# A fused two-layer decoder kernel: the shared LayerNorm steps of its Silu rounds and its last three Gelu visits are put in another order, and GpSimd takes part of the last tile's work

## The chip, the core and the metric

The kernel runs on one core of one Trainium2 chip. The metric is the device time in microseconds (us) of the whole program; before the change it is 501.37 us, the median of three runs (501.33 to 501.39). The core has TensorE (PE in the profile; its weight loads are PEld), VectorE (DVE), ScalarE (ACT), GpSimd (POOL) and SyncE (SP, which only issues DMAs). Each engine works through its own list of instructions in order, and the lists meet in semaphores: an instruction waits until a semaphore has reached a value, and whatever stands behind it on the same engine waits with it.

## The reference

The input is x of 8 x 56 tokens of width 256, a context of 8 x 1500 rows of width 256, and a mask over the context. All is in float32.

```python
x = x + L0_attn(layernorm(x))                # 16 heads of 128, ALiBi, causal
x = x + L0_xattn(layernorm(x), ctx, mask)    # 16 heads of 16 over 1500 rows, LayerNorm of the result
x = x + L0_ffn(layernorm(x))                 # ternary weights, 8-bit activations, silu(gate) * up, Hadamard
x = x + L1_attn(layernorm(x))                # attention over the batch axis: 16 query heads, 4 key heads of 16
x = x + L1_xattn(layernorm(x), ctx)          # LayerNorm(x5n + summary of a decaying scan) * gamma + beta
x = x + L1_ffn(layernorm(x))                 # 1024 wide, round(h / 0.1) clipped, gelu, power-of-two weights
```

Three of these matter here. `L0_ffn` is the one with the Silu. `L1_attn` attends from each of the 8 batch elements at one position to batch elements 0 to b; a token row forms products q x k over up to 8 batch elements, sums them in groups of 16, takes a softmax, and forms products p x v. `L1_xattn` is two LayerNorms in a row: x5 is normalised, the summary is added, that is normalised again, scaled by gamma (`rows_sb[:, 2]`), shifted by beta (`rows_sb[:, 3]`) and added to x.

## The kernel before, in words

The 448 tokens are four tiles of 112 rows (`TT`), each with two batch elements; the tiles are counted 0 to 3. After the first attention the kernel runs one long loop of 48 rounds, `s` = 0 to 47 (`PAIRS`), each for 250 rows of the context. A batch element takes 6 rounds, a tile 12. A round on PE is: scores (L1522), the key projection of a later piece (`project_k`, L1451), the weighted values of the round before (L1540), the value projection (`project_vu`, L1461). ACT takes the exponentials (L628) and most copies out of PSUM; DVE clips the exponentials (L998, `clip`), multiplies the context by the scan's weights (L972, `weigh`), and forms the remainder of each context piece (L832, `remainder`, in odd rounds), which the split float32 products need.

When a tile's 12 rounds are over, its other layers are worked in between the rounds of the next tiles. What belongs to round `o` behind a tile's end stands in small functions `first`, `early`, `between` and `late`, called from fixed places of the round: on ACT `first` comes right behind the exponential and the key copy, `early` further on, `late` last; on DVE `early` stands ahead of the clip, `between` behind it, `late` last.

Three rounds, 16, 28 and 40 (`SILU`), hold the Silu of one tile: ACT loads the Silu table, does the Silu, and loads back the table that has exponential and logarithm. To make room, DVE takes over copies that ACT otherwise does: the value copy (L1009), the rounding of a context piece (L827), and one round later (`BEHIND`, rounds 17, 29, 41) the key copy `take_k` (L1004). In rounds 28 and 40 the second LayerNorm chain of the tile before falls into the same place: `add_summary` on DVE (L1156 to L1159; its variance goes to ACT through `s_var[6]`), `root(6)` on ACT (an Ln and an Exp, L333 and L337), `add_normalised` on DVE (L1163, variance through `s_var[7]`), `root(7)` on ACT, and `normalise7` on DVE (L1168).

Behind round 47 comes the tail, written out by hand: rest of tile 2, all of tile 3, and the last layer of all tiles. It needs the Gelu table for tiles 0 and 1 together, for tile 2, and for tile 3, with the other table between. `keep_warm(n)` (L1731) issues n matmuls whose result nobody uses. Tile 0's last product (L1782, `hidden_part(0)`) waits for its Gelu; `turn_x7` (L1675) turns a tile's last normalised rows for the last layer, `hidden` is L1687, and tile 3's last two products are L1886 and L1893. In `spread` (L1094) and `attend` (L1131) DVE forms tile 3's products for all 8 batch elements, 256 elements for each.

## Time and profile before

| | |
|---|---|
| median of three runs | 501.37 us (501.33 to 501.39) |
| the profiled execution, its own time | 500.37 us |
| span of that execution, first to last instruction | 498.6 us |
| mean granted TensorE clock | 0.992 |
| PE busy | 475.3 us, 95% |
| DVE busy | 365.3 us, 73% |
| ACT busy | 321.6 us, 65% |
| POOL busy | 4.2 us, 1% |

All durations below come from that one execution. What lies outside its span is 1.8 us. A row of the time line gives the start from the span's beginning, the duration, engine, line, operation, what is written and read, and in brackets how long the engine stood idle before it and what ended that. Where several equal instructions are merged, the duration is from the start of the first to the end of the last.

### The profile page before, as it was taken

What the parts mean: (1) busy time and instruction counts of PE and PEld (TensorE: products, weight loads), DVE (VectorE), ACT (ScalarE), POOL (GpSimd) and SP (SyncE); (2) the same over time, 40 slices, a digit from 0 to 9 for tenths busy, and PEclk for the clock granted to TensorE, in tenths of its full rate; (3) what the DMA queues carried; (4) which work ended last, traced back from release to release, by engine and by line L of the source; (5) the groups of instructions that cost most, each with busy time, mean ns of one, the idle gap of its engine ahead of it and who ended that gap; (6) DMA issues with size and microseconds to landing.
All of it is one profiled execution on the core that took longest, in us unless ns stands there. A gap on an engine that the chain in (4) does not pass through costs nothing.

```text
span 498.6 us, 16397 instructions
## 1 busy us (share of the span) xinstructions
PE 475.3 (95%) x7061; PEld 406.9 (82%) x7067; DVE 365.3 (73%) x820; ACT 321.6 (65%) x591; POOL 4.2 (1%) x15
## 2 busy tenths in 40 slices
PE   7999999999989999999999999899999999896897
PEld 7999999999878888878888888788888788684575
DVE  5576887887658755567966579966969975798973
ACT  4677787877566666677566566666667556445644
POOL 1000000000000000000000000000000000000000
PEclk9999999999999999999999999999999999988999
DMA  6376452200501211111111111111111100000000
GB/s 201 108 254 203 168 166 84 64 23 28 206 1 45 79 50 44 44 44 44 44 44 44 44 44 44 44 44 44 42 44 44 44 3 3 3 1 0 1 11 28
DMA packets 12236, 30.86 MB, mean 62 GB/s; under 512 B 1666, under 2 KB 4867, under 8 KB 11396
## 3 DMA queue, kind: packets, MB, share of 16 engines
q1 hardware_dynamic: 11716, 29.08, 18.2%
q8 instruction: 56, 0.92, 0.7%
q0 software_dynamic: 192, 0.51, 0.3%
q10 hardware_dynamic: 256, 0.23, 0.1%
q14 instruction: 16, 0.13, 0.1%
HBM read 29.35 MB, written 0.46 MB: 60 GB/s over the span
## 4 chain that ended last, share of the span: by engine, by line
PE 69%; DVE 20%; ACT 5%; issue 4%; DMA 1%; DVEq 0%; ACTq 0%
PE psb L1461 10%; PE psb L1451 9%; PE psa L1370 8%; PE psa L1522 8%; PE psb L1540 6%; PE psa L1383 4%; PE pst L1392 4%; PE psb L1423 3%; PE psa L1403 2%; ACT shared L628 2%; DVE shared L998 1%; DVE st L782 1%; PE pst L1607 1%; DVE scratch L972 1%; PE psb L1414 1%
## 5 line engine op out<-in xcount | busy, mean ns | idle before, releaser
L1461 PE MATMUL psb<-wkv,cx 128*125 128x256 f32 x576 | 80.3, 288 | 2.7 <-DVE kx L1004 2.7
L1451 PE MATMUL psb<-cx,wkv 128*128 128x500 f32 x276 | 74.5, 405 | 0.8 <-ACT vmem L471 0.8
L1461 PEld LDWEIGHTS psb<-wkv,cx 128*125 128x125 f32 x576 | 71.0, 186 | 4.9 <-DVE kx L1004 3.0
L471 ACT ACTIVATE vmem<-psb 125x512 f32<-125x512 f32 x45 | 26.8, 596 | 50.1 <-PE psb L1461 49.8
L1451 PEld LDWEIGHTS psb<-cx,wkv 128*128 128x128 f32 x276 | 48.3, 188 | 12.6 <-ACT vmem L471 1.1
L1522 PE MATMUL psa<-qb,kx 32*125 32x112 f32 x1536 | 54.7, 279 | 0.8 <-ACT shared L628 0.6
L998 DVE TENSOR_SCALAR shared<-shared,top 125x896 f32<-125x896 f32 x48 | 30.8, 683 | 32.8 <-ACT shared L628 32.6
L1522 PEld LDWEIGHTS psa<-qb,kx 32*125 32x125 f32 x1536 | 46.3, 183 | 8.3 <-issue 3.5
L628 ACT ACTIVATE shared<-psa 125x1792 f32<-125x1792 f32 x24 | 40.0, 1668 | 17.4 <-PE psa L1522 17.2
L1370 PE MATMUL psa<-cx 128*128 128x448 f32 x192 | 44.5, 382 | 0.7 <-ACT cx L362 0.7
L628 ACT ACTIVATE smem<-psa 125x1792 f32<-125x1792 f32 x23 | 38.3, 1667 | 9.4 <-PE psa L1522 9.4
L998 DVE TENSOR_SCALAR smem<-smem,top 125x896 f32<-125x896 f32 x48 | 30.8, 681 | 16.5 <-ACT smem L628 16.0
L1370 PEld LDWEIGHTS psa<-cx 128*128 128x128 f32 x192 | 36.1, 195 | 3.8 <-DVE cx L797 1.0
L972 DVE CUSTOM_DVE_ANT_0 scratch<-ring,cw 128x500 f32<-128x500 f32 x48 | 32.3, 672 | 0.1
L377 ACT ACTIVATE shared<-shared,negmax 112x112 f32<-112x112 f32 x64 | 24.1, 377 | 10.0 <-DVE negmax L872 10.0
L832 DVE TENSOR_TENSOR cx<-ring,cx 128x1000 fp32r<-128x1000 f32 x24 | 28.7, 1194 | 2.5 <-ACT cx L393 2.0
L464 ACT ACTIVATE kx<-psb,cols_sb 128x500 f32<-128x500 f32 x43 | 28.8, 671 | 2.4 <-PE psb L1451 2.2
L1540 PEld LDWEIGHTS psb<-shared,vmem 125*32 125x32 f32 x1536 | 20.4, 110 | 8.5 <-issue 6.9
L1540 PEld LDWEIGHTS psb<-smem,vmem 125*32 125x32 f32 x1536 | 20.3, 110 | 8.0 <-issue 7.7
L1383 PE MATMUL psa<-wkv,cx 128*112 128x256 f32 x192 | 25.2, 280 | 0.0
L1383 PEld LDWEIGHTS psa<-wkv,cx 128*112 128x112 f32 x192 | 24.4, 174 | 0.7
L1540 PE MATMUL psb<-shared,vmem 125*32 125x56 f32 x1536 | 24.1, 214 | 0.3 <-DVE craw L989 0.3
(350 smaller groups left out, 833.7 us busy)
## 6 DMA issues: line engine op xcount, KB each, us to landing
ring<-ctx_t_dram SPq DMA_DIRECT2D x24, 500.0 KB, 3.4
whd<-wqk_dram SPq DMA_DIRECT2D x16, 256.0 KB, 2.7
qb<-wvp_dram SPq DMA_DIRECT2D x8, 256.0 KB, 2.8
whd<-wo_dram SPq DMA_DIRECT2D x16, 128.0 KB, 2.6
wraw<-w_dram SPq DMA_DIRECT2D x2, 1024.0 KB, 5.8
mats_sb<-mats_dram SPq DMA_DIRECT2D x1, 1536.0 KB, 8.1
wraw<-gate_dram SPq DMA_DIRECT2D x1, 1024.0 KB, 6.8
wraw<-up_dram SPq DMA_DIRECT2D x1, 1024.0 KB, 6.5
```

What stands on the lines that cost most here:

```text
L464: nc.scalar.activation(kx[u % 2][:, m, :], bank[:, 0:UT], ACT.Identity, bias=cols_sb[:, 1, m:m + 1]).then_inc(s_ke, 1)
L471: nc.scalar.activation(vu[u % 2][:, 2 * r:2 * r + 2, :, 0:XD], bank[0:CT, :].rearrange("p (t h d) -> p t h d", t=2, d=XD), ACT.Copy).then_ ...
L628: nc.scalar.activation(ex[s % 2], psa[0:CT, :, 0:448], ACT.Exp, scale=0.25).then_inc(s_ex, 1)
L832: nc.vector.tensor_tensor(cx[LO][u % 2][:, :, :], ctxs[u % 3], cx[HI][u % 2][:, :, :].bitcast(F32), ALU.subtract).then_inc(s_cx, 1)
L972: nc.vector.tensor_tensor_reduce(out=wscr[:, c, :], in0=ctxs[u % 3][:, c, :], in1=cw[:, (u % UPB) * UT:(u % UPB + 1) * UT], scale=1.0, sca ...
L998: nc.vector.tensor_scalar(half, half, top[:, pp // 2 // UPB, key:key + 1], 1.0 / ECLIP, ALU.min, ALU.max).then_inc(s_clip, 1)
L1370: last = nc.tensor.matmul(PS[0][:, part, 0:TOK], cq[a][h % 2][:, (c * 2 + part) * P:(c * 2 + part + 1) * P], x0[b][:, c, :], start=(a == b ...
L1383: last = nc.tensor.matmul(A2[0:TT, i * D:(i + 1) * D], x0[b][:, c, t * TT:(t + 1) * TT], wkv[a][:, j % 2, c, :], start=(a == b and c == 0) ...
L1451: last = nc.tensor.matmul(bank[:, 0:UT], wkv[a][:, 0, c, m * P:(m + 1) * P], cx[b][u % 2][:, c, :], start=(a == b and c == 0), stop=(a == ...
L1461: last = nc.tensor.matmul(bank[0:CT, t * D:(t + 1) * D], cx[b][u % 2][:, c, a0:a0 + CT], wkv[a][:, 1, c, :], start=(a == b and c == 0), st ...
L1522: last = nc.tensor.matmul(psa[0:CT, g, t * 224 + c * 112:t * 224 + (c + 1) * 112], kx[u % 2][32 * g:32 * g + 32, c, a0:a0 + CT], qb[32 * g ...
L1540: last = nc.tensor.matmul(pvb[32 * i:32 * i + 32, q * S:(q + 1) * S], vu[u % 2][:, 2 * r + t, 4 * q + i, :], ex[pp % 2][:, g, a0:a0 + S], ...
```

## The change

There are four parts.

1. In the loop, everything of the second LayerNorm chain is moved. On DVE `add_summary` goes from round offset 16 to 15 (from round 28 to 27 for tile 0, from 40 to 39 for tile 1), `add_normalised` from the end of round 28 to the end of round 27, and `normalise7` from ahead of the clip of round 29 to behind it. On ACT `root(6)` goes to `first` of round 27 and `root(7)` to `first` of round 29. In rounds 17, 29 and 41 `take_k` goes ahead of `remainder`.
2. In the tail on ACT the first Gelu visit holds tile 0 alone; tile 1's Gelu goes into the visit of tile 2, and tile 3's `root(5)` goes behind that visit. Tile 3's queries are copied to SBUF by ACT, and a step of tile 1's rounding comes earlier.
3. GpSimd forms batch elements 0 and 1 of tile 3's products, in `spread` and in `attend`, and adds beta for tile 2.
4. Of the matmuls that keep PE busy, 12 become 2 and 3 become 8.

```diff
+            pool.wait_ge(s_acc, 3)
+            pool.wait_ge(s_kve, 7)
+            nc.gpsimd.tensor_tensor(prod[:, 0:2 * D]..., q1[:, :]..., kv1[:, 0, 0:2, :]..., ALU.mult).then_inc(s_ones, 1)
+            pool.wait_ge(s_var[6], 3)
+            nc.gpsimd.tensor_tensor(xs[:, 2, :], xs[:, 2, :], rows_sb[:, 3, :], ALU.add).then_inc(s_ones, 1)
+            pool.wait_ge(s_sub, 5)
+            nc.gpsimd.tensor_tensor(prod[:, 0:2 * D]..., p1[:, 0:32]..., kv1[:, 1, 0:2, :]..., ALU.mult).then_inc(s_ones, 1)
...
             # ACT, first(t, o)
                 if o == 14:
                     root(5, t)
+                if o == 15:
+                    root(6, t)
+                if o == 17:
+                    root(7, t)
             # ACT, early(t, o) and late(t, o)
-                if o == 16:
-                    root(6, t)
...
-                if o == 16:
-                    root(7, t)
...
             # ACT, tail
+            act.wait_ge(s_qkv, 4)
+            nc.scalar.activation(q1[:, :], T1[0:TT, 0:D], ACT.Copy).then_inc(s_kve, 1)
+            act.wait_ge(s_zl, 2)
+            nc.scalar.activation(hz[1], hz[1], ACT.Relu, bias=low[:, 1:2], scale=-1.0).then_inc(s_zh, 1)
             act.wait_ge(s_qkv, 5)
             nc.scalar.activation(kv1[:, :, 6:8, :]...
             root(6, 2)
+            nc.scalar.preload_act_table(ACT.Gelu_apprx_tanh)
+            gelu(0)
             move_xbe(3)
-            act.wait_ge(s_zl, 2)
-            nc.scalar.activation(hz[1], hz[1], ACT.Relu, ...
             act.wait_ge(s_zh, 1)
             nc.scalar.activation(hz[1], hz[1], ACT.Identity, ...
+            back()
             act.wait_ge(s_var[6], 3)
             move_sy(3)
-            nc.scalar.preload_act_table(ACT.Gelu_apprx_tanh)
-            gelu(0)
-            gelu(1)
-            back()
             softmax_exp(3)
             root(7, 2)
+            nc.scalar.preload_act_table(ACT.Gelu_apprx_tanh)
+            gelu(1)
             move_x7T(2)
             move_h(2, 0)
             move_h(2, 1)
             move_aT(3)
-            root(5, 3)
-            nc.scalar.preload_act_table(ACT.Gelu_apprx_tanh)
             gelu(2)
             back()
+            root(5, 3)
             root(6, 3)
...
             # DVE: early, between, late, and the loop
-                if o == 16:
+                if o == 15:
                     add_summary(t)
-                if o == 17:
-                    normalise7(t)
...
+                if o == 17:
+                    normalise7(t)
...
-                if o == 16:
+                if o == 15:
                     add_normalised(t)
...
+                if s in BEHIND:
+                    take_k(s // 2 + 1, 1)
                 if s % 2 and s // 2 + 2 < B * UPB:
                     remainder(s // 2 + 2)
-                if s in BEHIND:
-                    take_k(s // 2 + 1, 1)
...
             # DVE, tail
-            dve.wait_ge(s_qkv, 4)
-            spread(3, 0, 6, T1[0:TT, 0:D])
-            dve.wait_ge(s_kve, 7)
-            spread(3, 6, 8, T1[0:TT, 0:D])
+            dve.wait_ge(s_kve, 8)
+            spread(3, 2, 8, q1[:, :])
+            dve.wait_ge(s_ones, 3)
             total(3, 0, 8)
...
             # PE, tail
-            keep_warm(12)
-            pe.wait_ge(s_kve, 7)
+            keep_warm(2)
+            pe.wait_ge(s_kve, 8)
             hidden_part(0, 0)
             hidden_part(0, 1)
-            keep_warm(3)
+            keep_warm(8)
             turn_x7(2)
```

The first place is ACT from round 27 into round 29, before the change. `lnv` and `y` are the Ln and the Exp of a root; `s_var6` and `s_var7` are the variances that DVE delivers; `gB` and `xqT` are tile 1's scale and quantised rows on their way to PE.

```order
L464 ACTIVATE kx<-psb,cols_sb 128x500 [waits s_qk,s_kp]
L507 ACTIVATE gB<-pst 128x112 [waits s_gb]
L503 ACTIVATE xqT<-pst 128x224 [waits s_xqt]
L471 ACTIVATE vmem<-psb 125x32x16 [waits s_pv,s_vp]
L628 ACTIVATE shared<-psa 125x1792 [waits s_pv,s_qk]
L464 ACTIVATE kx<-psb,cols_sb 128x500 [waits s_qk,s_kp]
L333 ACTIVATE lnv<-mv,eps 112x1 [waits s_var6]
L337 ACTIVATE y<-lnv 112x1 [waits s_act]
L510 ACT_TABLE_LOAD
L512 ACTIVATE whd<-whd 128x896 [waits s_gs]
L515 ACT_TABLE_LOAD
L333 ACTIVATE lnv<-mv,eps 112x1 [waits s_var7]
```

The same place of the changed kernel.

```order
L477 ACTIVATE kx<-psb,cols_sb 128x500 [waits s_qk,s_kp]
L346 ACTIVATE lnv<-mv,eps 112x1 [waits s_var6]
L350 ACTIVATE y<-lnv 112x1 [waits s_act]
L520 ACTIVATE gB<-pst 128x112 [waits s_gb]
L516 ACTIVATE xqT<-pst 128x224 [waits s_xqt]
L484 ACTIVATE vmem<-psb 125x32x16 [waits s_pv,s_vp]
L641 ACTIVATE shared<-psa 125x1792 [waits s_pv,s_qk]
L477 ACTIVATE kx<-psb,cols_sb 128x500 [waits s_qk,s_kp]
L523 ACT_TABLE_LOAD
L525 ACTIVATE whd<-whd 128x896 [waits s_gs]
L528 ACT_TABLE_LOAD
L641 ACTIVATE smem<-psa 125x1792 [waits s_pv,s_qk]
```

The root that waits for `s_var6` has moved ahead of the copies `gB` and `xqT`, and the exponential of round 29 (`smem<-psa`) now stands ahead of the root that waits for `s_var7`.

The second place is DVE from the end of round 28 into round 29, before the change; `vmem` is the value copy, `CAST cx` the rounding, `cx<-ring,cx` the remainder, `kx<-psb` is `take_k`.

```order
L1009 COPY vmem<-psb 125x32x16 [waits s_pv,s_vp]
L827 CAST cx<-ring 128x1000 [waits s_kp,s_cx,s_vp,s_ctx1]
L790 SCALAR_TENSOR_TENSOR yt<-y,nx 112x1 [waits s_rs6]
L792 SCALAR_TENSOR_TENSOR rs<-yt,y 112x1 [waits s_dve]
L1163 SCALAR_TENSOR_TENSOR xs<-wraw,rs,xs 112x256 [waits s_dve]
L782 BN_STATS st<-xs 112x6 [waits s_dve]
L783 BN_AGGR mv<-st 112x2 [waits s_dve]
L785 TENSOR_SCALAR nx<-mv 112x1 [waits s_var7]
L832 TENSOR_TENSOR cx<-ring,cx 128x1000 [waits s_ch,s_dve]
L1004 TENSOR_SCALAR kx<-psb,cols_sb 128x500 [waits s_qk,s_kp]
```

The same place of the changed kernel.

```order
L1024 COPY vmem<-psb 125x32x16 [waits s_pv,s_vp]
L842 CAST cx<-ring 128x1000 [waits s_kp,s_cx,s_vp,s_ctx1]
L1019 TENSOR_SCALAR kx<-psb,cols_sb 128x500 [waits s_qk,s_kp]
L847 TENSOR_TENSOR cx<-ring,cx 128x1000 [waits s_ch]
L1013 TENSOR_SCALAR smem<-smem,top 125x4x224 [waits s_ex]
```

Between the rounding and `take_k`, `add_normalised` (six instructions) is gone to the end of round 27, and the remainder now stands behind `take_k`.

## Rows read from the trace of the kernel before

**Rows 1.** The chain of waits that ended last, by engine (page).
```profile
PE 69%; DVE 20%; ACT 5%; issue 4%; DMA 1%; DVEq 0%; ACTq 0%
```
**Rows 2.** Time line, rounds 17 to 19: start us, us, engine, line, operation, [idle before].
```profile
235.11 1.20 DVE L832 TENSOR_TENSOR cx<-ring,cx 128x1000 fp32r<-128x1000 f32 x1
...
237.22 0.74 DVE L1004 TENSOR_SCALAR kx<-psb,cols_sb 128x500 f32<-128x500 f32 x1 [0.91 <-PE psb L1451]
...
246.68 0.39 DVE L989 COPY craw<-psb 128x224 f32<-128x224 f32 x1
...
247.43 0.99 PE L1540 MATMUL psb<-shared,vmem 125*32 125x56 f32 x64
```
**Rows 3.** Time line, rounds 27 to 31.
```profile
300.71 1.19 DVE L832 TENSOR_TENSOR cx<-ring,cx 128x1000 fp32r<-128x1000 f32 x1
...
301.16 0.36 ACT L503 ACTIVATE xqT<-pst 128x224 bf16<-128x224 bf16 x1 [0.30 <-PE pst L1573]
...
302.45 0.96 PE L1585 MATMUL pst<-xqT,wter 128*128 128x112 bf16 x16
...
304.61 0.21 DVE L790 SCALAR_TENSOR_TENSOR yt<-y,nx 112x1 f32<-112x1 f32 x1
...
306.03 0.18 DVE L783 BATCH_NORM_AGGREGATE mv<-st 112x2 f32<-112x6 f32 x1
...
309.82 0.67 DVE L827 CAST cx<-ring 128x1000 fp32r<-128x1000 f32 x1
...
310.35 1.62 PE L1451 MATMUL psb<-cx,wkv 128*128 128x500 f32 x6
...
312.05 0.29 ACT L333 ACTIVATE lnv<-mv,eps 112x1 f32<-112x1 f32 x1 [1.29 <-DVE mv L783]
...
312.48 1.20 DVE L832 TENSOR_TENSOR cx<-ring,cx 128x1000 fp32r<-128x1000 f32 x1 [0.28 <-DVE nx L785]
312.48 1.65 ACT L628 ACTIVATE smem<-psa 125x1792 f32<-125x1792 f32 x1
313.60 0.73 DVE L1004 TENSOR_SCALAR kx<-psb,cols_sb 128x500 f32<-128x500 f32 x1
...
314.38 1.69 PE L1461 MATMUL psb<-wkv,cx 128*125 128x256 f32 x12 [1.49 <-DVE kx L1004]
```
**Rows 4.** Time line, round 31.
```profile
323.83 0.38 DVE L989 COPY craw<-psb 128x224 f32<-128x224 f32 x1
...
324.26 0.99 PE L1540 MATMUL psb<-shared,vmem 125*32 125x56 f32 x64 [0.26 <-DVE craw L989]
```
**Rows 5.** Time line, tail: tile 3's products, the Gelu visits, the two turns.
```profile
460.62 0.38 ACT L691 ACTIVATE kv<-psb 112x256 f32<-112x256 f32 x1 [1.67 <-PE psb L1845]
...
463.37 2.75 PE L1731 MATMUL psb<-wter,identb 128*128 128x512 bf16 x12
...
465.59 1.79 ACT L580 ACTIVATE qb<-qb 128x896 f32<-128x896 f32 x2
...
471.35 0.41 PE L1675 MATMUL psa<-cst,scratch 112*128 112x112 f32 x2 [0.34 <-DVE scratch L1168]
...
482.67 3.71 PE L1782 MATMUL psa<-wraw,qb 128*112 128x256 f32 x16 [0.35 <-ACT qb L580]
...
487.68 0.41 PE L1675 MATMUL pst<-cst,wraw 112*128 112x112 f32 x2 [0.44 <-DVE wraw L1168]
```
**Rows 6.** Stretches of the tail: us, busy per engine, granted PE clock, DMA share, GB/s.
```profile
455.00:460.00 5.00, 4.27 (x18) 2.93 (x19) 3.46 (x13) 2.67 (x8) 0.00 (x0) 0.81 0.00 0
```
**Rows 7.** Time line: the same four matmuls early and late in the tail.
```profile
454.98 2.04 PE L1667 MATMUL psa<-proj_sb,xnT 128*112 128x256 f32 x4 [0.45 <-ACT xnT L558]
...
477.54 1.12 PE L1667 MATMUL pst<-proj_sb,xnT 128*112 128x256 f32 x4 [0.23 <-ACT xnT L558]
```
**Rows 8.** GpSimd's largest instruction, and a DVE product of 512 elements (time line).
```profile
123.28 0.95 POOL L318 MEMSET vmem<- 125x1024 f32 x1 [114.14 <-PE psa L1403]
...
474.78 0.69 DVE L1143 TENSOR_TENSOR wraw<-wraw 112x512 f32<-112x512 f32 x1
```

More of the change, by code:

```diff
@@ L320, in _ @@
             nc.gpsimd.memset(vu[1][:, :, :, XD:32], 1.0).then_inc(s_ones, 1)
+            pool.wait_ge(s_acc, 3)
+            pool.wait_ge(s_kve, 7)
+            nc.gpsimd.tensor_tensor(prod[:, 0:2 * D].rearrange("p (b r e) -> p b r e", r=4, e=64),
+                                    q1[:, :].rearrange("p (r e) -> p r e", r=4).unsqueeze(1).to_broadcast([TT, 2, 4, 64]),
+                                    kv1[:, 0, 0:2, :].unsqueeze(2).to_broadcast([TT, 2, 4, 64]), ALU.mult).then_inc(s_ones, 1)
+            pool.wait_ge(s_var[6], 3)
+            nc.gpsimd.tensor_tensor(xs[:, 2, :], xs[:, 2, :], rows_sb[:, 3, :], ALU.add).then_inc(s_ones, 1)
+            pool.wait_ge(s_sub, 5)
+            nc.gpsimd.tensor_tensor(prod[:, 0:2 * D].rearrange("p (m r d) -> p m r d", r=4, d=16),
+                                    p1[:, 0:32].rearrange("p (m r) -> p m r", r=4).unsqueeze(3).to_broadcast([TT, 8, 4, 16]),
+                                    kv1[:, 1, 0:2, :].rearrange("p b (k d) -> p (b k) d", d=16).unsqueeze(2).to_broadcast([TT, 8, 4, 16]),
+                                    ALU.mult).then_inc(s_ones, 1)
         @block.scalar
@@ L693, in _ @@
             root(6, 2)
+            nc.scalar.preload_act_table(ACT.Gelu_apprx_tanh)
+            gelu(0)
             move_xbe(3)
-            act.wait_ge(s_zl, 2)
-            nc.scalar.activation(hz[1], hz[1], ACT.Relu, bias=low[:, 1:2], scale=-1.0).then_inc(s_zh, 1)
             act.wait_ge(s_zh, 1)
             nc.scalar.activation(hz[1], hz[1], ACT.Identity, bias=low[:, 2:3], scale=-1.0).then_inc(s_z1, 1)
+            back()
             act.wait_ge(s_var[6], 3)
             move_sy(3)
-            nc.scalar.preload_act_table(ACT.Gelu_apprx_tanh)
-            gelu(0)
-            gelu(1)
-            back()
             softmax_exp(3)
             root(7, 2)
+            nc.scalar.preload_act_table(ACT.Gelu_apprx_tanh)
+            gelu(1)
             move_x7T(2)
@@ L1125, in weights @@
                 link(nc.vector.reciprocal(ri1[:, :], su1[:, :]))
-                link(nc.vector.tensor_tensor(pv, pv, ri1[:, :].unsqueeze(1).to_broadcast([TT, n, 16]), ALU.mult))
+                normal = nc.vector.tensor_tensor(pv, pv, ri1[:, :].unsqueeze(1).to_broadcast([TT, n, 16]), ALU.mult)
+                if t == 3:
+                    normal.then_inc(s_sub, 1)
+                    dve.wait_ge(s_sub, 5)
+                else:
+                    link(normal)
             def attend(t):
                 n = 2 * t + 2
-                link(nc.vector.tensor_tensor(prod[:, 0:n * D].rearrange("p (m r d) -> p m r d", r=4, d=16),
-                                             p1[:, 0:16 * n].rearrange("p (m r) -> p m r", r=4).unsqueeze(3).to_broadcast([TT, 4 * n, 4, 16]),
-                                             kv1[:, 1, 0:n, :].rearrange("p b (k d) -> p (b k) d", d=16).unsqueeze(2).to_broadcast([TT, 4 * n, 4, 16]),
+                f = 2 if t == 3 else 0
+                link(nc.vector.tensor_tensor(prod[:, f * D:n * D].rearrange("p (m r d) -> p m r d", r=4, d=16),
+                                             p1[:, 16 * f:16 * n].rearrange("p (m r) -> p m r", r=4).unsqueeze(3).to_broadcast([TT, 4 * (n - f), 4, 16]),
+                                             kv1[:, 1, f:n, :].rearrange("p b (k d) -> p (b k) d", d=16).unsqueeze(2).to_broadcast([TT, 4 * (n - f), 4, 16]),
                                              ALU.mult))
@@ L1138, in gather @@
                 if t == 3:
+                    dve.wait_ge(s_ones, 5)
                     link(nc.vector.tensor_tensor(prod[:, 0:4 * D], prod[:, 0:4 * D], prod[:, 4 * D:8 * D], ALU.add))
@@ L1158, in add_summary @@
                 link(nc.vector.scalar_tensor_tensor(out=x6u[t], in0=x5s[t], scalar=mean(6, t), in1=rows_sb[:, 2, :], op0=ALU.subtract, op1=ALU.mult))
-                link(nc.vector.tensor_tensor(xs[:, t, :], xs[:, t, :], rows_sb[:, 3, :], ALU.add))
+                if t != 2:
+                    link(nc.vector.tensor_tensor(xs[:, t, :], xs[:, t, :], rows_sb[:, 3, :], ALU.add))
             def add_normalised(t):
                 polish(6, t)
+                if t == 2:
+                    dve.wait_ge(s_ones, 4)
                 link(nc.vector.scalar_tensor_tensor(out=xs[:, t, :], in0=x6u[t], scalar=col(rs, 6, t), in1=xs[:, t, :], op0=ALU.mult, op1=ALU.add))
```

## The prediction

> **What bounds the kernel now.** I read three views, in this order. First the chain of waits that ended last [rows 1]: PE carries 69% of it, but DVE a fifth, though DVE is busy for only 73% of the span. So DVE bounds in some stretches. Then the list of who waited for whom, and the time line where that list pointed. In most rounds PE never stops. In the Silu rounds 28 and 40 it does: the value projection starts at 314.38, having stood 1.49 us for DVE's key copy [rows 3]. ACT stands 1.29 us for the variance of `add_normalised` there. A round and a half later PE again stands for a DVE copy, 0.26 us for `craw` [rows 4]. From the clip of round 27 to that copy DVE has next to no gap; the one row with an idle mark on it is 0.28 us [rows 3]. The reader is to see that DVE's own backlog sets when PE may go on at 324.26, so that any idle time put into DVE's list ahead of 323.83 comes out on PE. Last the tail: the turn of tile 2 at 471.35 and of tile 3 at 487.68 both wait for DVE, by 0.34 and 0.44 us [rows 5].
>
> **Part 1a: remainder behind the key copy, round 17.** Before, DVE does the remainder at 235.11 for 1.20 us, and then still stands 0.91 us for PE's key projection; the key copy starts at 237.22 [rows 2]. In the new order the key copy comes first and the remainder fills no gap any more: it starts at the copy's end, so everything behind it is 1.20 - 0.08 = 1.12 us later (0.08 is how far two DVE instructions overlap: 300.71 + 1.19 is 301.90, and the next one starts at 301.82 in the same list). I find no gap on DVE between 237.96 and `craw` at 246.68. That copy ends at 247.07 and PE's weighted values start at 247.43, which PE's own work allowed; a semaphore takes about 0.06 us from DVE to PE, so 0.30 us of slack are there. PE is 1.12 - 0.30 = 0.82 us late. Nothing on PE up to round 27 waits for anybody long enough to win it back. Loss: 0.82 us.
>
> **Part 1b: rounds 27 to 31, and 39 to 43.** I work it on the old time axis, as if 1a had not happened.
> - `add_summary` needs 1.60 us from its first instruction at 304.61 to the end of its BN_AGGR at 306.21 [rows 3]. In the new order it begins when the remainder is done, at 301.82. The variance is there at 303.42.
> - ACT's `root(6)` stands ahead of `gB` and `xqT` now, so ACT stands from about 300 to 303.45. A root lasts 0.43 us to the start of what follows (312.05 to 312.48), and `gB` with `xqT` 0.6 more. `xqT` ends at about 304.45 in place of 301.52. PE's gate product, which started at 302.45 without waiting, starts at 304.50: 2.05 us late, and scores, exponential and key projection of round 28 with it.
> - DVE meanwhile has enough to do. Its old list from 301.82 to the end of the rounding at 310.49 is 8.67 us without a gap; `add_normalised` joins it. From the end of the rounding to 312.20, where the remainder's 0.28 us of idle time began, that is 1.71 us, plus 0.08 of overlap. So the rounding ends at 301.82 + 8.67 + 1.79 = 312.28.
> - Next on DVE is the key copy, and the key projection that it reads ended at 310.35 + 1.62 = 311.97 before and ends at 314.02 now. DVE stands 1.8 us at a place where it had none, with the remainder, the clip and `normalise7` queued behind the waiting copy. All of DVE's work up to `craw` is the same, so `craw` is 1.8 us later, and PE at 324.26 was waiting for just that [rows 4]. I count 1.85, with the hop to DVE. The 0.28 us of idle time ahead of the old remainder may or may not be won.
> - What the edit wins is real but shorter: ACT no longer stands 1.29 us for `s_var7`, and PE no longer 1.49 us for the key copy. These two pay back the 2.05 us on the exponential of round 29, which comes about when it came before. On DVE they pay nothing.
> The same rows stand 77 us later for tile 1. Loss: 2 x 1.85 = 3.7 us.
>
> **Part 2 and 4: the tail up to the turn of tile 2.** Before, tile 0's product waits for the first Gelu, which ends near 465.59 + 0.95 = 466.54. Now ACT does a query copy and a step of tile 1 first, so the key copy slips from 460.62 to about 460.96; then 0.28 to its end less overlap, a root (0.43), a table load (1.28, an unlisted but constant length in this trace) and one Gelu (0.95): 464.0. Two copies of 0.6 together, PE's output projection of 1.3 and two idle-filling matmuls of 0.23 each (2.75 / 12) follow: tile 0's product begins near 466.3, some 0.4 earlier than before. Behind it stand 8 such matmuls in place of 3, 5 x 0.23 = 1.15 more. PE was ready to turn tile 2 at 471.35 - 0.34 = 471.01, and is now at 471.01 - 0.4 + 1.15 = 471.7: 0.3 us later than the turn was. DVE is 1.2 us ahead there, and hidden by the 8 matmuls.
>
> **Part 3: GpSimd.** Nothing in the trace multiplies on GpSimd. From below, the product of 512 elements takes what DVE needs, 0.69 us [rows 8]. From above, a memset writes 1024 elements in 0.95; with two operands to read besides, three times 0.93 ns for each of 512 is 1.4 us, and twice that, 2.8, is my far end, since the operands are broadcast in four dimensions. I take 1.4, being nearest to a row of GpSimd's own. The first product can start at 460.2 and is wanted by the sum over the products at about 463.1; the third has the 0.6 us of `normalise7` and DVE's own 1.76 us product beside it. At 1.4 both are hidden, at 2.8 the first nearly so.
> The Trainium skill (GPSIMD Engine Reference, Performance versus the Vector engine) gives 4497 ns for an add of 2048 elements; a quarter of that is an estimate of 1.1 us, and the sum would be the same by it. No run here shows it yet.
>
> **Part 2, end of the tail.** Tile 2's Gelu no longer waits behind a root and a table load, so PE's product at 482.67 does not wait its 0.35 us, and the table is back 1.3 us sooner for `root(6)` of tile 3. `root(5)` is 0.4 later, `root(6)` about 1.5 earlier. DVE has tile 3's rows ready near 486.6; PE, 0.3 late but without the two waits (0.35 and 0.44) and the stop ahead of the second block, can turn at 486.9 in place of 487.68. From there all is as before [rows 5]. Net of the tail: -0.8 us.
>
> **The clock.** With 12 filling matmuls down to 2, PE stands about 2.8 us in one piece, from 461.8 to 464.6 of the old axis, and does little for 5 us. The trace shows the granted clock falling to the lower level (1.2 GHz) after such thin stretches: the mean is 0.81 over 455 to 460 [rows 6], after a wait of 2.65 us near 449 to 451.4. Four 128x256 matmuls take 2.04 us there and 1.12 at 2.4 GHz [rows 7], 0.23 each. If such a stretch falls on tile 0's product, and covers six or seven of its matmuls, it costs 1.5 us; part may fall into the gap. PE sets the turn of tile 2 now, so it is all on the path. I take 1.0.
>
> **Sum.** 0.82 + 3.7 - 0.8 + 1.0 = +4.7 us on the profiled execution's 500.37, so 505.1; its time lies 1.0 under the median of the runs, so on that 501.37 + 4.7 = 506.1 us.
>
> **The rivals.**
> - No lower clock in the new gap: 505.1. For it: from 457 on the clock stayed at full speed. Against: no gap of 2.8 us was there to test it.
> - DVE held up by GpSimd. From this kernel's rows: the tail's DVE work beside the first product and the beta is a chain, and if DVE cannot start a two-operand instruction while GpSimd runs, it loses up to the first product and the add, 1.4 + 0.7 = 2.1 us; DVE is 1.2 ahead, and PE leaves another 0.4. That is 0.5 on the path, and with products of 2.8 us up to 1.9: 506.6 to 508.0, say 507.3. The Trainium skill (SBUF — State Buffer, two separate sides) has such a rule: DVE with two SBUF inputs and a GpSimd instruction that reads SBUF take one port pair in turns, and the later one "fully blocks". Nothing before the change could show it.
> - Half of part 1b is absorbed, because a later wait of PE (0.7 us for ACT near 399) swallows it: 506.1 - 1.0 - 1.8 = 503.3.
> - The other side: the waits that the edit removes are gone and nothing takes their place. Then PE gains 1.49 and 1.2 in the two rounds and 0.8 in the tail: 501.4 - 3.5 = 497.9. This decides at one point, whether the variance is there before `xqT` is due at 301.16. Against it: DVE finishes its remainder only at 301.90 and needs 1.60 more.
> - The loop's loss is covered and the tail's gain too: no change.
>
> **Chances.** Forecast 0.47 (505.3 to 507.2 by itself), no lower clock 0.20, port 0.13, half absorbed 0.10, faster 0.06, no change 0.04. 0.2% is about what a measurement of this kernel can tell from none. Faster by over that 0.06, within it 0.04, slower by over it 0.90. The range of 503.3 to 508.1 leaves out the last two cases and the far end of the port.
>
> **What would show it.** In the changed profile, ACT's `lnv` of round 27 stands some 3 us for DVE's `mv`, and the gate product starts late behind `xqT`; ACT no longer waits ahead of the exponential of round 29; DVE stands nearly 2 us ahead of `take_k` in rounds 29 and 41 and 2 us in 17; the `craw` copy behind them (246.68 and 323.83 here, and its like in the third round) comes about 1.1, 2.7 and 4.5 us late; the first turn of the tail follows the filling matmuls and not DVE. I am wrong if `gB` and `xqT` are on time, if the exponential of round 46 is under 3 us late, or if the tail gives back more than 2 us.

## The result, and the profile after

| | before | changed |
|---|---|---|
| median | 501.35 us (4 runs, 500.87 to 501.39) | 506.69 us (4 runs, 504.58 to 508.90) |
| profiled execution, own time | 500.37 us | 505.50 us |
| span | 498.6 us | 503.7 us |
| busy PE, DVE, ACT, POOL | 475.3, 365.3, 321.6, 4.2 us | 474.9, 365.7, 321.6, 7.5 us |

The ratio is 1.0109, 95% interval 1.0060 to 1.0159: slower by 5.5 us (3.0 to 8.0). The forecast was 506.1 us, that is +4.7. Two runs of the experiments below were far slower than the rest (889 us of `loop_only` and 1546 us of `loop_old_take`) and are left out of every median, ratio and range. No engine has more work apart from GpSimd, so the time is waiting. The chain that ended last, by engine, has hardly moved against [rows 1]:

```profile
PE 69%; DVE 20%; ACT 6%; issue 3%; DMA 1%; SPq 0%; DVEq 0%; ACTq 0%
```

Shares of a chain do not tell two versions apart here. What does is one event of every round set side by side, the start of the exponential on ACT, and in the tail the distance from the last of them:

| | before | changed | later by |
|---|---|---|---|
| exponential of round 0 | 143.35 | 144.24 | 0.89 |
| round 16 | 229.75 | 231.21 | 1.46 |
| round 20 | 252.89 | 255.18 | 2.29 |
| round 26 | 292.60 | 294.86 | 2.26 |
| round 28 | 304.54 | 308.82 | 4.28 |
| round 29 | 312.48 | 314.77 | 2.29 |
| round 32 | 329.73 | 333.54 | 3.81 |
| round 38 | 369.42 | 373.24 | 3.82 |
| round 46 | 418.32 | 423.72 | 5.40 |
| turn of tile 2, from round 46 | 53.03 | 53.97 | 0.94 |
| turn of tile 3, from round 46 | 69.36 | 69.06 | -0.30 |

So the loop loses three times, 0.83 us (rounds 16 to 20), 1.56 (26 to 38) and 1.58 (38 to 46), the tail is 0.30 shorter, and 1.46 us are there before the first instruction that the change touches. Of these, 0.89 lie ahead of the loop. The two executions differ there in the granted clock from 5 to 15 us (the column behind the last bracket; first before, then changed):

```profile
5.00:15.00 10.00, 8.29 (x49) 7.25 (x49) 5.20 (x16) 5.62 (x12) 1.76 (x3) 1.00 0.76 243
5.00:15.00 10.00, 7.55 (x43) 6.33 (x43) 5.32 (x16) 5.20 (x11) 1.81 (x3) 0.68 0.77 249
```

No edit of this document touches anything in that stretch, and eight of the fourteen kept profiles show the clock at its lower level (1.2 GHz) for part of it. Their loops start 0.65 to 0.89 us behind that of before; of the five others at full clock three start at most 0.37 behind it, and two 1.23 and 1.38. Time line of the changed kernel, round 17 and what follows:

```profile
238.68 0.74 DVE L1019 TENSOR_SCALAR kx<-psb,cols_sb 128x500 f32<-128x500 f32 x1 [2.14 <-PE psb L1475]
...
249.70 0.99 PE L1564 MATMUL psb<-shared,vmem 125*32 125x56 f32 x64 [0.74 <-DVE craw L1004]
```

In [rows 2] DVE stood 0.91 us ahead of this key copy, with the remainder done; now 2.14, and PE stands 0.74 us at the weighted values where it had no wait. Rounds 27 to 31, against [rows 3] and [rows 4]:

```profile
305.74 0.29 ACT L346 ACTIVATE lnv<-mv,eps 112x1 f32<-112x1 f32 x1 [3.50 <-DVE mv L798]
...
306.72 0.96 PE L1609 MATMUL pst<-xqT,wter 128*128 128x112 bf16 x16 [1.85 <-ACT xqT L516]
...
313.93 0.67 DVE L842 CAST cx<-ring 128x1000 fp32r<-128x1000 f32 x1
...
316.29 0.74 DVE L1019 TENSOR_SCALAR kx<-psb,cols_sb 128x500 f32<-128x500 f32 x1 [1.69 <-PE psb L1475]
...
320.72 0.33 SPq L296 DMA_DIRECT2D ring<-ctx_t_dram  x1
...
324.13 1.04 ACT L406 ACTIVATE cx<-ring 128x1000 fp32r<-128x1000 f32 x1 [1.96 <-DMA ring<-ctx_t_dram]
...
325.95 1.62 PE L1475 MATMUL psb<-cx,wkv 128*128 128x500 f32 x6 [0.71 <-ACT vmem L484]
...
327.64 0.39 DVE L1004 COPY craw<-psb 128x224 f32<-128x224 f32 x1
...
328.08 0.99 PE L1564 MATMUL psb<-shared,vmem 125*32 125x56 f32 x64 [0.50 <-DVE craw L1004]
```

Read it downwards. ACT stands 3.50 us for the variance, the gate product is late behind it (PE stands 1.85 us), DVE stands ahead of the key copy, and PE pays in two places: 0.50 us for the `craw` copy (0.26 in [rows 4]), as forecast, and ahead of that 0.71 us for the value copy `vmem`, for which it had no wait. That copy stood on ACT behind the rounding of a context piece, which waited 1.96 us for its DMA; SP had issued that DMA at 320.72, when DVE's `weigh` of round 29 was done. Idle time on DVE is passed on by the loads too.

The tail, against [rows 5] and [rows 7]:

```profile
460.00 1.12 PE L1691 MATMUL psa<-proj_sb,xnT 128*112 128x256 f32 x4 [0.45 <-ACT xnT L571]
...
464.86 1.30 POOL L324 TENSOR_TENSOR wraw<-q,kv 112x512 f32<-112x512 f32 x1 [331.15 <-ACT q L704]
465.47 0.97 DVE L1180 SCALAR_TENSOR_TENSOR scratch<-scratch,mv,rows_sb 112x256 f32<-112x256 f32 x1
...
466.11 0.92 POOL L328 TENSOR_TENSOR xs<-xs,rows_sb 112x256 f32<-112x256 f32 x1
...
466.48 2.16 DVE L1109 TENSOR_TENSOR wraw<-q,kv 112x1536 f32<-112x1536 f32 x1
...
469.23 0.43 PE L1881 MATMUL psa<-bias,minus 2*112 2x256 f32 x1 [2.82 <-ACT xnT L555]
469.59 2.05 PE L1883 MATMUL psa<-mats_sb,xnT 128*112 128x256 f32 x4
471.43 1.06 PE L1755 MATMUL psb<-wter,identb 128*128 128x512 bf16 x2
472.28 3.85 PE L1806 MATMUL psb<-wraw,qb 128*112 128x256 f32 x16
...
474.72 1.11 DVE L805 SCALAR_TENSOR_TENSOR yt<-y,nx 112x1 f32<-112x1 f32 x1
474.76 1.05 POOL L330 TENSOR_TENSOR wraw<-p,kv 112x512 f32<-112x512 f32 x1 [7.74 <-DVE p L1141]
...
476.19 1.67 PE L1755 MATMUL psb<-wter,identb 128*128 128x512 bf16 x7
...
477.69 0.36 PE L1699 MATMUL psa<-cst,scratch 112*128 112x112 f32 x2
```

Three DVE instructions are longer while GpSimd works. The scaling by gamma takes 0.97 us (0.48 at 488.67 in the same execution), the product of six batch elements 2.16 (1.75 for the like one at 476.39), and a step on a single element per row 1.11 (0.22 at 491.86). That is 1.8 us. PE's turn of tile 2 does not wait for it: it follows the filling matmuls with no idle time, 1.2 us after DVE has its rows ready (476.06 + 0.41). The four matmuls at the lower clock, which were L1667's in [rows 7], are now L1883's. In both kernels the clock falls once in this part of the tail, at different places (stretches of before, then of the changed kernel):

```profile
450.00:460.00 10.00, 7.08 (x37) 4.61 (x39) 7.87 (x23) 6.08 (x14) 0.00 (x0) 0.83 0.00 0
460.00:475.00 15.00, 13.49 (x79) 9.39 (x79) 14.19 (x26) 9.87 (x17) 0.00 (x0) 1.00 0.00 1
...
455.00:467.00 12.00, 7.84 (x50) 5.18 (x51) 10.20 (x29) 8.71 (x20) 2.14 (x2) 1.00 0.00 0
467.00:475.00 8.00, 5.77 (x19) 4.06 (x20) 7.55 (x15) 6.42 (x11) 0.26 (x2) 0.79 0.00 1
```

How far tails differ by themselves can be read as well: nine kept profiles, two of before and seven of the experiments below, have the old tail. From the exponential of round 46 their turn of tile 2 comes at 52.19 to 53.03 us and that of tile 3 at 68.52 to 69.36. The first profile of before is the latest of the nine in both. So the -0.30 of the last row of the table lies within what tails with the same code differ by, while the turn of tile 2 at 53.97 does not.

### The profile page after: what moved, and what is told of

Same layout as the page of the kernel before. It is cut to its first block, busy times and chain, and to the rows that moved or that the text cites. A ratio compares the mean times of both kernels' runs of the same rounds, so it can differ in the third digit from the quotient of the medians.

```text
span 503.7 us, 16392 instructions
## 1 busy us (share of the span) xinstructions
PE 474.9 (94%) x7056; PEld 406.9 (81%) x7062; DVE 365.7 (73%) x818; ACT 321.6 (64%) x592; POOL 7.5 (1%) x18
## 4 chain that ended last, share of the span: by engine, by line
PE 69%; DVE 20%; ACT 6%; issue 3%; DMA 1%; SPq 0%; DVEq 0%; ACTq 0%
PE psb L1475 9%; PE psb L1485 9%; PE psa L1546 8%; PE psa L1394 7%; PE psb L1564 6%; PE psa L1407 4%; PE pst L1416 3%; PE psb L1447 3%; PE psa L1427 2%; ACT shared L641 2%; DVE shared L1013 1%; PE psa L1806 1%; DVE scratch L987 1%; DVE cx L847 1%; PE pst L1609 1%
## 5 line engine op out<-in xcount | busy, mean ns | idle before, releaser
L406 ACT ACTIVATE cx<-ring 128x1000 fp32r<-128x1000 f32 x21 | 21.8, 1038 | 7.2 <-DMA ring<-ctx_t_dram 7.1
```

## The experiments

All twelve were timed with before on the same chip; ratios come with their 95% interval, and the differences in us are the ratio applied to the median of before beside them, so they can be some tenths off the difference of the medians. That is 500.77 us for `loop_only`, `tail_only`, `loop_old_take` and `loop_root6_behind`, 501.00 for `before_again`, `warm_moved`, `warm_moved_no_pool` and `gpsimd_probe`, and 500.46 for the other four. "Theory A" is mine after the result: idle time that gets into DVE's list ahead of the `craw` copy is the loss. "Theory B" is that the late gate product is.

**Part 1 alone** (`loop_only`).

> The kernel before with part 1 alone (the loop's moves on ACT and DVE), the tail as before. Theory A, idle time in DVE's list: DVE stands ahead of take_k in rounds 17, 29 and 41 and what it loses comes out on PE behind the craw copy. The profile of the changed kernel shows 0.83, 1.56 and 1.57 us of it, so this kernel is 3.9 to 4.1 us slower than before, 505.3, and its runs agree within 0.5 us. Theory B, the late gate product: ACT's root stands 3.5 us ahead of gB and xqT, the gate products of rounds 27 and 39 come 2.05 us late, and this is what is lost; it gives the same 4 us here and is told apart by the next two kernels. A rival on the scatter: if the loop makes the changed kernel's runs differ by 4 us, it shows here.

Measured: 505.06 us, ratio 1.0093 (1.0072 to 1.0113), +4.7 us (3.6 to 5.7), five runs from 504.9 to 506.4. Its trace has 0.79, 1.55 and 1.58 us in the three places. The loop is nearly the whole of the result.

**Parts 2 to 4 alone** (`tail_only`).

> The kernel before with parts 2, 3 and 4 alone (Gelu visits, GpSimd's share, filling matmuls), the loop as before. Theory: the tail makes the scatter of the changed kernel (504.6 to 508.9 us), by stretches of the lower clock that fall differently from run to run, since its PE stands 2.8 us in one piece where 12 filling matmuls were. Then the runs of this kernel lie between 500.6 and 504.9 us, with the lower mean clock in the longer ones, median some +1 us. Rival: the tail is worth a steady -0.6 us (500.7), its runs within 0.5 us, and the scatter is the loop's.

Measured: 502.25 us, 1.0024 (1.0011 to 1.0037), +1.2 us, runs from 500.3 to 503.1. Its trace has the turn of tile 3 68.91 us behind the exponential of round 46, 0.45 sooner than before's first profile and in the middle of the nine old tails, and yet the runs are slower: what they lose is in part open (below). The tail's scatter of 2.9 us is less than the changed kernel's 4.3 and more than part 1's 1.5, so it does not explain the changed kernel's by itself.

**The order of take_k and remainder** (`loop_old_take`), part 1 with

```diff
-                if s in BEHIND:
-                    take_k(s // 2 + 1, 1)
                 if s % 2 and s // 2 + 2 < B * UPB:
                     remainder(s // 2 + 2)
+                if s in BEHIND:
+                    take_k(s // 2 + 1, 1)
```

> Part 1 alone, but with the remainder ahead of take_k as before the change in rounds 17, 29 and 41. Theory A: the remainder (1.20 us) fills most of the idle time that DVE has ahead of take_k, nothing is lost in round 17, and some 0.7 us each in rounds 27 to 31 and 39 to 43: +1.4 us, 502.8. Theory B: the gate products are as late as before this edit, and only round 17's 0.83 us are gone: +3.1 us, 504.5.

Measured: 503.24 us, 1.0057 (1.0036 to 1.0079), +2.9 us (1.8 to 4.0). By the time alone this is B's number, +3.1, and not A's, +1.4. The trace shows what it is made of. DVE in round 29 of this kernel:

```profile
313.01 1.20 DVE L832 TENSOR_TENSOR cx<-ring,cx 128x1000 fp32r<-128x1000 f32 x1
314.67 0.74 DVE L1004 TENSOR_SCALAR kx<-psb,cols_sb 128x500 f32<-128x500 f32 x1 [0.45 <-PE psb L1451]
```

The idle time is down from 1.69 to 0.45 us, and rounds 17 and 27 to 31 lose 0.01 and 0.44 us, though the gate product of round 27 is as late as ever. That is A. The third place, where A expected 0.7, loses 1.81 (rounds 38 to 46): DVE stood 0.46 us there too, but ACT waited 2.79 us for the context piece in round 42 (1.71 in before), and PE 1.61 for ACT (0.52).

```profile
400.62 1.04 ACT L393 ACTIVATE cx<-ring 128x1000 fp32r<-128x1000 f32 x1 [2.79 <-DMA ring<-ctx_t_dram]
```

That wait is no fixed quantity: in the six profiles whose loop has before's code it is 1.71, 1.43, 2.27, 1.42, 2.23 and 2.42 us, and the length of rounds 38 to 46 differs by up to 1.0 us among them. So the third place is a rough measure, and the second one carries the argument.

**root(6) behind the copies** (`loop_root6_behind`). On ACT `root(6, t)` goes from `first` to `early`, where tile t + 1's gB and xqT come ahead of it.

> Part 1 alone, but root(6) of rounds 27 and 39 behind the copies gB and xqT on ACT, so that the gate products are on time; take_k stays ahead of the remainder. Theory A: round 17 costs 0.82 us as before, and DVE still stands ahead of take_k by 1.1 to 1.3 us in rounds 29 and 41, so most of the loss is left: +3.2 us, 504.6. Theory B: with the gate product on time the loss of rounds 27 to 31 and 39 to 43 is gone and only round 17's 0.8 us are left: 502.2.

Measured: 503.74 us, 1.0057 (1.0035 to 1.0079), +2.9 us (1.8 to 4.0), against +3.2 by A and +0.8 by B. The exponential of round 28 is on time and DVE still stands:

```profile
315.03 0.74 DVE L1004 TENSOR_SCALAR kx<-psb,cols_sb 128x500 f32<-128x500 f32 x1 [1.13 <-PE psb L1451]
```

B as the whole cause is ruled out. Rounds 27 to 31 lose 0.99 us in place of 1.55, so the late gate product does have its part, by the idle time that it makes on DVE.

**Both** (`both_undone`).

> Part 1 alone, with root(6) behind gB and xqT and with the remainder ahead of take_k: what is left of part 1 is that the second LayerNorm chain is one round earlier. Theory A, two causes that add up on DVE (idle time ahead of take_k from the order, and from the late gate product): with both gone 0.2 us are left, within 0.2% of before. Rival: the earlier chain itself costs, since it fills DVE ahead of the Silu rounds, and 1 us or more is left.

Measured: 501.07 us against 500.46, 1.0012 (1.0001 to 1.0023), +0.6 us (0.05 to 1.15). Its trace loses nothing in rounds 17 and 27 to 31 (0.10 us are won), and 1.19 in rounds 38 to 46, where ACT waited 2.70 us for the context piece. A's 0.2 us lies in the interval, the rival's 1 us at its upper end: moving the chain a round earlier costs little by itself, and whether a few tenths of it are real is not settled.

**Filling the idle time with something else** (`loop_weigh_ahead`), part 1 with

```diff
                 if s in BEHIND:
+                    weigh(s // 2, s % 2)
                     take_k(s // 2 + 1, 1)
...
-                weigh(s // 2, s % 2)
+                if s not in BEHIND:
+                    weigh(s // 2, s % 2)
```

> Part 1 alone as it is, with DVE's weigh of rounds 17, 29 and 41 (0.75 us) in the idle time ahead of take_k. Theory A: idle time in DVE's list is the loss, so each round gives back 0.7 us, and the load of the next context piece, which is issued when that weigh is done, starts some 3 us earlier, so that ACT's rounding in rounds 18, 30 and 42 waits for no DMA: +2.4 us against before, 503.3 with before at 500.9, and the wait for the ring tile on ACT gone. Theory B (the late gate product): no change against part 1 alone, +4.7.

Measured: 503.20 us, 1.0057 (1.0035 to 1.0078), +2.8 us (1.8 to 3.9), against +2.4 by A and +4.7 by B. Round 17 loses 0.09 us in place of 0.79, and ACT waits for no context piece in rounds 18, 30 and 42. So A holds. The profiled run (504.1) shows something else beside it, the granted clock after PE's wait for `xqT`. The stretches (length, then busy PE, PEld, DVE, ACT and POOL, granted clock, DMA share, GB/s), and under them the gate product, which takes 0.96 us elsewhere:

```profile
304.00:310.00 6.00, 4.66 (x53) 4.13 (x54) 5.62 (x16) 2.38 (x6) 0.00 (x0) 0.72 0.25 79
310.00:314.00 4.00, 4.00 (x103) 3.43 (x105) 3.06 (x7) 3.95 (x5) 0.00 (x0) 1.00 0.05 17
```
```profile
305.34 1.62 PE L1587 MATMUL pst<-xqT,wter 128*128 128x112 bf16 x16 [1.84 <-ACT xqT L503]
```

So the late gate product can have a second price: in this execution the clock is at its lower level (1.2 GHz) for part of the stretch behind it, and the exponential of round 29 comes 1.6 us later than in part 1 alone, measured from round 26. Part 1 alone and the changed kernel, profiled with the same wait, had 1.00 there.

**A wait of PE that is worth nothing** (`take_first_later`): before, with `take_k` ahead of `remainder` in rounds 29 and 41.

> The kernel before, with take_k ahead of the remainder in rounds 29 and 41 alone. The key copy then comes 1.1 us earlier, and PE does not stand 1.49 and 1.2 us for it. Theory A, DVE's backlog: DVE's list up to the craw copy is as long as before, so PE stands at the craw copy what it no longer stands at the value projection, and the program is the same within 0.3 us. Rival: the wait for the key copy is a loss of its own, and the program is 1.5 to 2.4 us faster.

Measured: 500.70 us, 1.0007 (0.9992 to 1.0022): no change, where 1.5 to 2.4 us faster was the rival. In its trace, of the slowest of its twelve runs (503.24), rounds 27 to 31 take what they took before to 0.05 us: PE's wait for the key copy fell from 1.49 to 0.42 us, and the one for `craw` rose from 0.26 to 0.45, with 0.76 for `vmem` ahead of it.

```profile
315.23 1.68 PE L1463 MATMUL psb<-wkv,cx 128*125 128x256 f32 x12 [0.42 <-DVE kx L1004]
...
324.14 1.63 PE L1453 MATMUL psb<-cx,wkv 128*128 128x500 f32 x6 [0.76 <-ACT vmem L471]
...
326.21 0.99 PE L1542 MATMUL psb<-shared,vmem 125*32 125x56 f32 x64 [0.45 <-DVE craw L989]
```

**The kernel before once more** (`before_again`).

> The kernel before, unchanged. Its runs in the last comparison went from 499.4 to 502.2 us. Theory: what tail_only lost against before (+1.2 us) is more than two copies of one program differ by, so this one is within 0.4 us of before (500.3 to 501.2 with before at 500.8). Rival: two copies of one program can differ by 1 us as well, and then no difference of that size says anything of an edit. Its profile shows whether the start of the loop (exponential of round 0) at 143.4 us, which no changed kernel reached (144.0 to 144.2), was a lucky one.

Measured: 500.46 us, 0.9992 (0.9978 to 1.0005). Its loop starts at 144.58, 1.23 us later than in the first profile of the same program, and ends 1.03 later. So 1.46 us ahead of round 16 need no cause in the change: 0.89 of them come ahead of the loop, and the rest, nearly all in rounds 2 to 4, stands in the profiles of `both_undone` and `take_first_later` too, which leave these rounds as they were.

**The filling matmuls** (`warm_moved`): the changed tail, `keep_warm(12)` ahead of `pe.wait_ge(s_xbe, 8)` in place of 2, and `keep_warm(3)` ahead of `turn_x7(2)` in place of 8.

> The loop of before with the changed tail, but 12 filling matmuls stand ahead of tile 3's summary product, where PE stands 2.8 us now, and 3 behind tile 0's product in place of 8. Theory: the gap is what lowers the clock over the summary product and tile 0's product (2.05 us for four matmuls that take 1.12 otherwise), and the 8 matmuls are what sets the turn of tile 2, since DVE has its rows ready 1.2 us before it. So the turn comes 1.2 to 2 us earlier, and the program ends 1.1 us or more ahead of tail_only: 501.1 if that is 502.2. Rival: the clock falls all the same, or DVE is no earlier, and this is within 0.3 us of tail_only.

Measured: 500.91 us, 1.0002 (0.9990 to 1.0015), while `tail_only` had 1.0024. The lower clock is gone from that place (it is back where before has it, 32 to 40 us behind the exponential of round 46), the turn of tile 2 comes 0.44 us sooner than in `tail_only` where 1.2 to 2 were expected, and now it waits for DVE, whose one-element step stands behind GpSimd:

```profile
465.32 1.12 PE L1883 MATMUL psa<-mats_sb,xnT 128*112 128x256 f32 x4
...
470.55 1.11 DVE L805 SCALAR_TENSOR_TENSOR yt<-y,nx 112x1 f32<-112x1 f32 x1
470.59 1.05 POOL L330 TENSOR_TENSOR wraw<-p,kv 112x512 f32<-112x512 f32 x1 [7.74 <-DVE p L1141]
...
472.35 0.41 PE L1699 MATMUL psa<-cst,scratch 112*128 112x112 f32 x2 [1.39 <-DVE scratch L1193]
```

**GpSimd's work given back to DVE** (`warm_moved_no_pool`).

> warm_moved, with GpSimd's two products and its addition given back to DVE. Theory, a shared port: while GpSimd works, DVE's instructions with two operands in SBUF stand (0.97 for 0.48, 2.16 for 1.75 and 1.11 for 0.22 us in the profile of the changed kernel, together 1.8 us), which is more than the 0.44 + 0.42 us of work that GpSimd takes from DVE ahead of tile 2's last rows. Without GpSimd DVE has those rows 0.9 us earlier, and the program is 0 to 0.9 us faster than warm_moved, by how far DVE sets the turn. Rival: GpSimd's work is gained time, and without it the rows come 0.9 us later and the program with them.

Measured: 498.89 us, 0.9965 (0.9952 to 0.9979), -1.75 us: faster than before. From the last exponential to the turn of tile 2 it takes 52.47 us, against 53.38 with GpSimd: the 0.9 us that was worked out from the three lengthened instructions. The runs of the two kernels are 1.85 us apart, twice that; what the rest is the two profiles do not show.

**The port by itself** (`gpsimd_probe`), before with

```diff
+            pool.wait_ge(s_acc, 1)
+            for i in range(40):
+                pool.wait_ge(s_ones, 2 + i)
+                nc.gpsimd.tensor_tensor(q1[:, :], rows_sb[:, 0, :], rows_sb[:, 1, :], ALU.add).then_inc(s_ones, 1)
...
+                if t == 1:
+                    act.wait_ge(s_ones, 42)
```

The second addition keeps ACT from writing `q1` before the last of the forty is done; no wait of ACT for GpSimd shows in the trace.

> The kernel before, and GpSimd adds two SBUF rows of 256 elements 40 times in a row, from the end of round 24 on, into a tile that nobody reads then. Theory, a shared port: in that stretch DVE's instructions with two SBUF operands (weigh, 0.67 us; the remainder, 1.19; the products) are up to 0.6 us longer, and those with one (the clip, 0.64; the copies) are not; GpSimd's own additions last longer too while DVE has two operands. DVE then bounds rounds 25 to 31, and the program is 2 to 10 us slower. Rival: no instruction of DVE is longer, GpSimd's additions last 0.65 us each, and the program is the same.

Measured: 511.09 us, 1.0211 (1.0197 to 1.0225), +10.6 us for 35.3 us of GpSimd's additions. Not all of it need be DVE's longer instructions: PE waits in these rounds, and its granted clock is 0.67 over 300 to 310 us and 0.66 over 320 to 330, where before has 1.00. DVE by shape between 285 and 315 us; behind the bar busy time and ns of one:

```profile
L1004 DVE TENSOR_SCALAR smem<-smem,top 125x896 f32<-125x896 f32 x4 | 4.4, 1138 | 1.4 <-ACT smem L634 1.4
L978 DVE CUSTOM_DVE_ANT_0 scratch<-ring,cw 128x500 f32<-128x500 f32 x3 | 3.1, 1041 | 0.0
...
L788 DVE BATCH_NORM_STATS2 st<-xs 112x6 f32<-112x256 f32 x2 | 0.9, 428 | 0.1
...
L1154 DVE TENSOR_TENSOR xs<-xs,pst 112x256 f32<-112x256 f32 x1 | 0.4, 408 | 0.0
```

The same in before:

```profile
L972 DVE CUSTOM_DVE_ANT_0 scratch<-ring,cw 128x500 f32<-128x500 f32 x4 | 2.7, 673 | 0.0
...
L998 DVE TENSOR_SCALAR smem<-smem,top 125x896 f32<-125x896 f32 x4 | 2.6, 682 | 1.6 <-ACT smem L628 1.6
...
L782 DVE BATCH_NORM_STATS2 st<-xs 112x6 f32<-112x256 f32 x3 | 1.3, 427 | 0.1
```

`weigh`, with two operands in SBUF, goes from 673 to 1041 ns. The clip, with one, goes from 682 to 1138, which I had not expected. The statistics (one operand) and the addition with one operand in PSUM are not lengthened (427 and 428; 421 before, 408). The Trainium skill (SBUF — State Buffer, two separate sides) names both kinds that are held up, DVE operations with two SBUF inputs and those in a two-port performance mode, and says that the one that starts second "fully blocks". The trace agrees, with 1.11 us for a step of 0.22 beside 1.05 us of GpSimd, both ending at 475.8. Which of the two started first it does not show, their records begin 0.04 us apart. That the clip runs in such a mode is my reading of it. The clip's time fits it, 0.76 ns for an element (682 for 896) against 1.20 ns in the two-operand remainder [rows 2], but the mode itself was not measured.

**A version that beats both** (`combined`): the loop of before with

```diff
+                if s in BEHIND[1:]:
+                    take_k(s // 2 + 1, 1)
...
-                if s in BEHIND:
+                if s in BEHIND[:1]:
                     take_k(s // 2 + 1, 1)
...
+                if s in BEHIND:
+                    weigh(s // 2, s % 2)
                 clip(s)
...
-                weigh(s // 2, s % 2)
+                if s % 12 == 6 and s > 12:
+                    take_raw(s // 6 - 1)
+                if s not in BEHIND:
+                    weigh(s // 2, s % 2)
...
-                if s % 6 == 0 and s:
+                if s % 6 == 0 and s and not (s % 12 == 6 and s > 12):
                     take_raw(s // 6 - 1)
```

and the tail of `warm_moved_no_pool` with `keep_warm(1)` ahead of `turn_attended(3)`.

> A candidate that beats both kernels: the loop of before with take_k ahead of the remainder in rounds 29 and 41, weigh of rounds 17, 29 and 41 ahead of the clip (so that the next context piece is loaded 1.3 us earlier), the craw copy of rounds 18, 30 and 42 ahead of weigh; and the tail of warm_moved_no_pool with 1 filling matmul in place of 4 ahead of tile 3's turn. Theory: the reordering takes 0.7 us off each of rounds 29 to 33 and 41 to 46, since the craw copy that PE waits for no longer stands behind weigh, and the tail 0.2: 1.6 us under warm_moved_no_pool, 3.2 under before. Rival: PE waits for the clip in place of the craw copy, and this is within 0.4 us of warm_moved_no_pool.

Measured: 497.84 us against 500.46, 0.9949 (0.9933 to 0.9964), -2.6 us (-3.4 to -1.8), runs from 497.3 to 498.6, where -3.2 was expected. It beats both kernels. Against `warm_moved_no_pool` it gains 0.8 us of the 1.6 expected, and the two intervals overlap. By the traces the loop is 0.7 us shorter than before's from round 26 to 32 and 1.0 from 38 to 46, where ACT's wait for the context piece is 0.74 us.

## Why the prediction was right, point by point

- **Part 1a**, 0.82 us: 0.83 in the trace. DVE's wait of 2.14 us was forecast as 2. Right in mechanism and size.
- **Part 1b**, 1.85 us twice: 1.56 and 1.58. The gate product came 2.01 us late (306.72 against 302.45, less the 2.26 that were there before) where 2.05 was forecast, DVE's wait was 1.69 against 1.8, and the exponential of round 29 was back at its old distance (2.29 against 2.26 ahead of it), as was said. The way it reaches PE was only half told: the prediction had the `craw` copy alone, and the traces show the load of the context piece, issued by the same late DVE, ACT's rounding and the `vmem` copy ahead of it. The size is 0.3 smaller mainly because DVE's old idle time of 0.28 us ahead of the remainder is gone, which the prediction had left open. Moving each half back shows that the two add: in rounds 27 to 31, 0.44 us are left of 1.55 with the old order of `take_k`, 0.99 with the gate product on time, and nothing with both. The third place does not show this as cleanly (1.81, 1.01 and 1.19 us are left), because the wait for the context piece in round 42 differs from execution to execution. The rival of the half-absorbed loss rested on a wait of PE near 399 us; it is 0.52 us and not 0.7 (that is the weight load's), and nothing was absorbed there.
- **The tail**, -0.8 + 1.0 = +0.2 us: -0.30 in the trace, and the changed tails (69.06 and 68.91 us) lie in the middle of the nine old ones, so that no gain is shown. The turn of tile 2 is 0.94 us later (0.3 and the clock's 1.0 were forecast), bound by the 8 filling matmuls and not by DVE, and from there to the turn of tile 3 1.24 us are won (1.1 forecast). The stretches are right, and their sum is as small as was said.
- **The clock**, +1.0 us: as a difference against before this term failed. The gap of 2.82 us came and the lower clock came behind it. It cost 1.57 us on PE's way to the turn: 2.05 us for L1883's four matmuls (1.12 in before), 1.06 for two filling ones (0.59) and 3.85 for the product (3.68). But the stretch that had cost L1667's four 2.04 in place of 1.12 in [rows 7] was gone. It moved and was not added. All nine profiles with the old tail have the lower clock somewhere from 32 to 40 us behind the exponential of round 46, and none has it from 44 to 50; the changed kernel and `tail_only` have it the other way round. The argument that the clock of before stayed at full speed from 457 us on holds only to 490: over the last stretch it was 0.89.
- **The port rival**, 0.13: its mechanism is true, 1.8 us of DVE's time, and its price on the path in this kernel is nought, because the lower clock and the 8 filling matmuls keep PE busy 1.2 us longer than DVE. In `warm_moved`, with the gap filled and 3 matmuls there, it was on the path, with 0.9 us.
- **The sum** came out well partly by luck. The terms as the trace has them make 0.83 + 1.56 + 1.58 - 0.30 = 3.7 us, against 4.7 forecast. The profiled execution was 5.1 longer because 1.46 lie ahead of anything changed, a difference that two executions of before show as well. The runs say +4.7 (3.6 to 5.7) for the loop and +1.2 (0.55 to 1.85) for the tail.

**Open.** Why the tail alone is slower in its runs when its profiled execution is not. The granted clock that each run lists gives a part. In before's three sets the runs with a mean clock of 0.986 are on average 0.7 to 1.1 us longer than those with 0.997 of the same set. Beside `tail_only`, two of 22 runs of before have 0.986 and none less, six have 0.997; of `tail_only`'s twelve, seven have 0.986 or less and none 0.997. That is not all of it, since its three runs with 0.990 are still 1.8 us above before's eleven with 0.990. Whether the tail makes the lower clock more frequent is not shown; a part of it, from 5 to 15 us, lies ahead of everything that was changed. The other thing that differs is the wait for the context piece in round 42, 1.42 to 2.42 us in executions with before's loop.

The scatter of the changed kernel goes with the clock too: 504.58 and 505.50 us at 0.986, 507.89 at 0.980, 508.90 at 0.983. A lower clock behind a long wait of PE in the loop, as in `loop_weigh_ahead`, would do this, but no profile of one of the two long runs exists, and part 1 alone, with the same two waits, stayed within 504.9 to 506.4.

## What to carry to other kernels

Find the engine whose backlog sets when the bounding engine may go on, and guard its list: an instruction that waits for something not yet there delays all that stands behind it, the loads that hang on it included. Where that list is what the bounding engine waits for next, the idle time becomes time of the program (1.69 us became 1.56 here), and a piece of ready work moved into the gap wins it back. A visible wait of the bounding engine was worth nothing to remove where that list got no shorter: 1.07 us less for the key copy gave nothing. Before work is given to GpSimd, add up the DVE instructions beside it, even the one-element ones. And before a price is put on a lower clock, look whether the kernel pays it already somewhere else.
